# A DLRM tower on one core: gathers paced by a count of products, a fourth one-hot unit, fourteen units as pairs

## The chip, the cores and the metric

One core of one Trainium2 chip runs the whole program. The metric is the device time in microseconds (us), median of three runs.

## The reference, cut to what matters

```python
e = jnp.stack([tbl_f[ids[:, f]] for f in range(40)], axis=1)   # 512 x 40 x 64, float32
vi, vj = e[:, i_idx, :], e[:, j_idx, :]                        # all 780 pairs i < j
z = jnp.einsum('bpe,bpe->bp', jnp.einsum('bpd,pde->bpe', vi, W), vj)
h = jnp.concatenate([z, dense_ctx], axis=1)                    # 780 + 16
h = jnp.maximum(h @ W_top1 + b_top1, 0.0)                      # 512
h = jnp.maximum(h @ W_top2 + b_top2, 0.0)                      # 256
y = h @ W_top3
```

40 embedding tables, batch 512, 64 numbers a row. For each of the 780 pairs of fields, one field's vector goes through that pair's 64x64 matrix and is multiplied with the other's and summed. All is float32.

## The kernel before, in words

**Units and duos.** Two fields make a unit; `x[:, u, :]` holds unit u with its 2 x 64 numbers on the partitions and the batch along the row. The plan cuts the pairs into 196 duos, four to a round, 49 rounds (0 to 48). A duo is two 64-row matmuls side by side (TensorE, L443, written as four instructions; "four" duos at L434 as eight), a product by VectorE (L380, or L375 and L377 for a "four") into `prod`, and later a sum over partitions by TensorE (`sum_round`, L464) into `z_ps`. `sum_round` of a round comes two rounds late (`LAG`). Rounds 0 to 16 are pair rounds; from round 17 come the quad rounds, whose factor is `x_quad`, made by four ScalarE copies (L309) for each unit from `PAIRED` = 12 on. Rounds 23 and 39 are mixed ones. Each unit is made at a fixed duo (`transposed_at`): units 3 to 13 at duos 3, 7, 11, 16, 22, 30, 38, 47, 57, 60, 64, then 84, 88, 116, 120, 148, 152.

**How a unit is made.** Units 0 to 2 (`HOT_FIELDS`, small tables) come from one-hot products ahead of duo 0: VectorE compares the ids with the row numbers (L351, eight times for a unit), TensorE multiplies table and one-hot (L397, 32 instructions a unit) into `t_ps`, ScalarE copies it to `x` (L301). All three use the one bank `t_ps`, so each waits for the copy of the one before. The other 17 units are gathered: eight indirect DMAs of 128 rows for each, issued by GpSimd (L262), then four transposes (L411) into `t_ps` and the same copy.

**What sets GpSimd's order.** Its queue is written by hand. First it issues the gathers of units 3 to 15 one after the other, and at the first gather of a unit waits that the unit before has landed, and from unit 7 on that the slot of four is free (L261). From round 19 (`first_shared`) it issues two gathers for each round, and in 21 rounds (`plan.added`: 20, 22, 24, 26, 28, 30, 32, 34 to 38, 40 to 48) it adds products in pairs (L282, two instructions a round), after which `sum_round` takes four matmuls instead of eight.

**The rest.** SyncE loads the ids, the one-hot ids (`hot_ids_sb`, 512 KB a unit, by broadcast), `ident`, then the weights of every round (256 KB, eight slots; L242), from the third round on behind the first `x_ready`. ScalarE's queue loads the tables of the one-hot units (256 KB for each field, L290) and small things. At the end TensorE sums the last rounds, runs layer 1 (L474), layer 2 (L509) and the output (L515).

Of the kernel before, what the change touches and what calls it, by code (L numbers as in the profile page):

```python
# [6 lines left out]
I32 = mybir.dt.int32  # L7
# [6 lines left out]
DIM = 64  # L14
BATCH = 512
# [10 lines left out]
PROD_SLOTS = PROD_ROUNDS * ROUND  # L26

LAG = 2
GATHER_SLOTS = 4
W_SLOTS = 8  # L30

PAIRED = 12
QUADS = (UNITS - PAIRED) // 2
BLOCK_ROUNDS = QUAD // 4
DENSE_AT = 104

GATHERS_A_ROUND = 2


def pair_index(i, j):  # L40
# [1 line left out]

HOT_FIELDS = [2, 3, 4, 12, 17, 24]
HOT_UNITS = len(HOT_FIELDS) // 2

LANES = 128
HOT_SLOTS = 3
FIELD_ORDER = HOT_FIELDS + [f for f in range(FIELDS) if f not in HOT_FIELDS]  # L50


# [4 lines left out]
class Plan:  # L57
# [7 lines left out]
    def __init__(self):  # L65
        pairs = []
        for u in range(PAIRED):
            pairs += [("pair", k, u) for k in range(u)]
            if u % 4 == 3:
                pairs.append(("four", u - 3, u))  # L70
        full = len(pairs) // ROUND
        self.rounds = [pairs[i * ROUND:(i + 1) * ROUND] for i in range(full)]
        self.quad_start = []
        inside = pairs[full * ROUND:]
        for c in range(QUADS):
            u = PAIRED + 2 * c
# [16 lines left out]
        self.first_shared = self.quad_start[1] - 4  # L93

        left = CHUNKS * 2 * (UNITS - PAIRED - 4)
        self.added = []
        for r in range(self.first_shared, len(self.rounds)):
            left -= GATHERS_A_ROUND
            if self.is_quad(r) and (left <= 0 or (r - self.first_shared) % 2):
                self.added.append(r)  # L100

    def is_quad(self, r):
        return self.rounds[r][0][0] == "low"
# [40 lines left out]
def dlrm_tower(nc, ids, hot_ids, lane_rows, tables, w1_in, w2_in, head_in, dense_in, w_in, identity, selector, out):  # L144
# [7 lines left out]
    with ExitStack() as ctx:  # L152
# [13 lines left out]
        hot_ids_sb = sb("hot_ids_sb", [LANES, HOT_UNITS, 2, BATCH], I32)  # L166
        lane_rows_sb = sb("lane_rows_sb", [LANES, per_lane])
        hot_tables = sb("hot_tables", [LANES, HOT_UNITS, 2, per_lane * DIM])
# [4 lines left out]
        hot = x_quad[0:LANES, 2 * (QUADS - HOT_SLOTS):2 * QUADS, :]  # L173
# [5 lines left out]
        head = sb("head", [ROWS, M1 + 2 * M2])  # L179
        y_row = sb("y_row", [1, BATCH])  # L180

        h1 = [prod[:, m // 2, m % 2, :] for m in range(M1)]
        h2 = [prod[:, M1 // 2 + m // 2, m % 2, :] for m in range(M2)]
        b1, b2, w3 = head[:, 0:M1], head[:, M1:M1 + M2], head[:, M1 + M2:M1 + 2 * M2]
# [1 line left out]
        y_ps = psum("y_ps", [ROWS, DUO_SLOTS, 2, BANK])  # L186
        z_ps = psum("z_ps", [ROWS, BANK])
        t_ps = psum("t_ps", [ROWS, BANK])
        h1_ps = [t_ps[:, :], y_ps[:, 0, 0, :], y_ps[:, 0, 1, :], y_ps[:, 1, 0, :]]
        h2_ps = [y_ps[:, 1, 1, :], y_ps[:, 2, 0, :]]  # L190
        out_ps = y_ps[0:1, 2, 1, :]
# [5 lines left out]
        head_loaded = sem("head_loaded")  # L197
        w1_loaded = sem("w1_loaded")
        dense_loaded = sem("dense_loaded")
        lane_rows_loaded = sem("lane_rows_loaded")  # L200
        hot_ids_loaded = [sem(f"hot_ids_loaded{u}") for u in range(HOT_UNITS)]
        hot_tables_loaded = [sem(f"hot_tables_loaded{u}") for u in range(HOT_UNITS)]
# [22 lines left out]

        @block.sync
        def _(sp):
            sp.dma_start(ids_sb[:, :, :], ids).then_inc(ids_loaded, 16)
            for u in range(HOT_UNITS):
                sp.dma_start(hot_ids_sb[:, u, :, :],  # L230
                             hot_ids[u:u + 1, :, :].broadcast_to([LANES, 2, BATCH])).then_inc(hot_ids_loaded[u], 16)
                if u == 0:
                    sp.dma_start(ident[:, :], identity).then_inc(ident_loaded, 16)
            for r in range(len(plan.rounds)):
                slot = r % W_SLOTS
                if r == 2:

                    sp.wait_ge(x_ready, 1)
                if r >= W_SLOTS:

                    sp.wait_ge(y_ready, ROUND * (r - W_SLOTS + 1))
                sp.dma_start(w[:, slot, :, :], w_in[:, ROUND * r:ROUND * (r + 1), :]).then_inc(w_loaded[slot], 16)  # L242
            sp.wait_ge(out_ready, 1)
            sp.dma_start(out.rearrange("b o -> o b"), y_row[:, :]).then_inc(out_stored, 16)
            sp.wait_ge(out_stored, 16)

        @block.gpsimd
        def _(pool):
            pool.wait_ge(ids_loaded, 16)

            def gather(g):
# [15 lines left out]
            gathers = 2 * CHUNKS * UNITS  # L267
            g = 2 * CHUNKS * HOT_UNITS
            while g < 2 * CHUNKS * (PAIRED + 4):
                gather(g)  # L270
                g += 1
            for r in range(plan.first_shared, len(plan.rounds)):
                for _ in range(GATHERS_A_ROUND):
                    if g < gathers:
                        gather(g)
                        g += 1
# [7 lines left out]

        @block.scalar
        def _(act):
            act.dma_start(lane_rows_sb[:, :], lane_rows).then_inc(lane_rows_loaded, 16)
            for u in range(HOT_UNITS):
                for s, f in enumerate(fields_of(u)):
                    act.dma_start(hot_tables[:, u, s, :],  # L290
                                  tables[f]).then_inc(hot_tables_loaded[u], 16)
# [4 lines left out]
            def save_x(u):  # L296
                if u < HOT_UNITS:
                    act.wait_ge(hot_used, per_lane * (u + 1))
                else:
                    act.wait_ge(unit_transposed, u - HOT_UNITS + 1)  # L300
                nc.scalar.copy(x[:, u, :], t_ps[:, :]).then_inc(x_ready, 1)  # L301

                if u >= PAIRED:

# [37 lines left out]
        def _(dve):  # L342
            dve.wait_ge(lane_rows_loaded, 16)
            for u in range(HOT_UNITS):
                dve.wait_ge(hot_ids_loaded[u], 16)
                for q in range(per_lane):
                    n = per_lane * u + q
                    if n >= HOT_SLOTS:

                        dve.wait_ge(hot_used, n - HOT_SLOTS + 1)  # L350
                    nc.vector.tensor_scalar(hot[:, 2 * (n % HOT_SLOTS):2 * (n % HOT_SLOTS) + 2, :], hot_ids_sb[:, u, :, :],  # L351
                                            lane_rows_sb[:, q:q + 1], None, ALU.is_equal).then_inc(hot_ready, 1)
            have = {"x": 0, "quads": 0}
            for d, (kind, k, c) in enumerate(plan.duos):
# [31 lines left out]
        @block.tensor  # L386
        def _(pe):
            def pick_unit(u):
                pe.wait_ge(hot_tables_loaded[u], 32)
                if u:  # L390

                    pe.wait_ge(x_ready, u)
                for q in range(per_lane):
                    n = per_lane * u + q
                    pe.wait_ge(hot_ready, n + 1)
                    for s in range(2):
                        last = nc.tensor.matmul(t_ps[s * DIM:(s + 1) * DIM, :],  # L397
                                                hot_tables[:, u, s, q * DIM:(q + 1) * DIM],
                                                hot[:, 2 * (n % HOT_SLOTS) + s, :], start=q == 0, stop=q == per_lane - 1)
                    last.then_inc(hot_used, 1)  # L400

            def transpose_unit(u):
# [183 lines left out]
```

## Time and profile before

| | us |
|---|---|
| runs (three) | 389.33, 386.92, 388.93; median 388.93 |
| the profiled execution | 383.91 |
| its span, first to last instruction | 382.1 |
| TensorE busy | 339.4 (89%) |
| VectorE busy | 252.1 (66%) |
| GpSimd busy | 230.0 (60%) |
| ScalarE busy | 41.5 (11%) |

The span leaves out 1.8 us of the profiled execution. TensorE's records start when an instruction is handed to the engine, and their ends are modelled, so its busy time is no proof that it worked all that while. Idle time of an engine is put down to the engine that released it; "remote" stands where the profile shows no work that ended just before.

### The profile page before, as it was taken

To read this page: it belongs to the slowest core of one execution; us is meant where nothing else is said; L and a number is where in the kernel's file an instruction comes from. 1 tells how busy PE (TensorE), PEld (TensorE's weight loads), DVE (VectorE), ACT (ScalarE), POOL (GpSimd) and SP (SyncE) were. 2 spreads that over 40 slices of the span, in tenths; PEclk is the share of its full clock that TensorE was granted. 3 is DMA by queue.
4 is the path that set the end of the run, shared out by engine and by line. 5 is a ranking of instruction groups with operands and counts; after the bars stand their busy time and mean duration, and the time that the engine had idled before them with its cause. 6 is when DMAs were issued, how large, how long until landed. Compare 5 with 4: busy or idle time off the path is not lost.

```text
span 382.1 us, 4042 instructions
## 1 busy us (share of the span) xinstructions
PE 339.4 (89%) x1656; PEld 116.1 (30%) x1656; DVE 252.1 (66%) x225; ACT 41.5 (11%) x67; POOL 230.0 (60%) x182
## 2 busy tenths in 40 slices
PE   1999889886786398869999999999999999999997
PEld 0334223221221122312333233333333333333442
DVE  2686867664344276637887999889998999991000
ACT  1001000000000000312006000330006000001022
POOL 5586666766666651650017768878899499994000
PEclk9999999995868779998999999999999999999999
DMA  7551323222211273211211122222211210000000
GB/s 244 196 188 21 77 50 79 52 54 48 52 48 24 54 268 91 50 21 55 57 55 44 54 48 64 70 70 69 62 43 48 57 28 2 0 0 2 0 0 0
DMA packets 13764, 23.33 MB, mean 61 GB/s; under 512 B 3489, under 2 KB 3873, under 8 KB 13618
## 3 DMA queue, kind: packets, MB, share of 16 engines
q1 hardware_dynamic: 7778, 14.57, 13.0%
q0 software_dynamic: 4352, 4.47, 5.6%
q10 hardware_dynamic: 1616, 4.04, 3.0%
q8 instruction: 13, 0.21, 0.2%
q14 instruction: 5, 0.04, 0.0%
HBM read 23.06 MB, written 0.00 MB: 60 GB/s over the span
## 4 chain that ended last, share of the span: by engine, by line
PE 78%; POOL 7%; DVE 6%; another core or an unknown queue 4%; issue 3%; DMA 2%; ACT 0%; ACTq 0%; DVEq 0%
PE y_ps L443 41%; PE z_ps L464 18%; POOL prod L282 7%; PE t_ps L397 6%; PE y_ps L474 5%; DVE prod L380 4%; PE t_ps L411 2%; PE y_ps L434 2%; PE y_ps L509 2%; DMA hot_tables<-in_tbl 2%; PE t_ps L474 2%; DVE prod L377 1%; DVE prod L375 1%; PE y_ps L515 0%
## 5 line engine op out<-in xcount | busy, mean ns | idle before, releaser
L443 PE MATMUL y_ps<-x,w 64*128 64x512 f32 x768 | 190.5, 626 | 29.2 <-DVE prod L380 16.6
L262 POOL DMA_INDIRECT gathered<-in_tbl,ids_sb x136 | 131.8, 969 | 70.5 <-issue 35.7
L380 DVE TENSOR_TENSOR prod<-y_ps,x_quad 128x1024 f32<-128x1024 f32 x120 | 138.5, 1217 | 16.5 <-PE y_ps L443 14.5
L282 POOL TENSOR_TENSOR prod<-prod 128x1024 f32<-128x1024 f32 x42 | 98.0, 2359 | 47.7 <-DVE prod L380 47.1
L380 DVE TENSOR_TENSOR prod<-y_ps,x 128x1024 f32<-128x1024 f32 x72 | 84.9, 1220 | 60.2 <-PE y_ps L443 31.0
L443 PEld LDWEIGHTS y_ps<-x,w 64*128 64x128 f32 x768 | 69.4, 190 | 138.2 <-issue 93.2
L464 PE MATMUL z_ps<-prod,select 128*32 128x512 f32 x616 | 81.7, 639 | 0.2 <-POOL prod L282 0.2
L464 PEld LDWEIGHTS z_ps<-prod,select 128*32 128x32 f32 x616 | 15.6, 113 | 60.6 <-issue 45.8
L301 ACT COPY x<-t_ps 128x512 f32<-128x512 f32 x20 | 11.7, 585 | 200.3 <-PE t_ps L411 84.2
L397 PE MATMUL t_ps<-x_quad,hot_tables 128*64 128x512 f32 x96 | 23.5, 646 | 9.6 <-DMA hot_tables<-in_tbl 8.1
L351 DVE TENSOR_SCALAR x_quad<-hot_ids_sb,lane_rows_sb 128x1024 f32<-128x1024 int32 x24 | 18.3, 773 | 12.9 <-DMA hot_ids_sb<-hot_ids 7.2
L309 ACT COPY x_quad<-x 32x512 f32<-32x512 f32 x32 | 19.7, 616 | 0.5
L474 PE MATMUL y_ps<-zT,w 128*128 128x512 f32 (+1 forms) x42 | 18.5, 594 | 0.0
L397 PEld LDWEIGHTS t_ps<-x_quad,hot_tables 128*64 128x64 f32 x96 | 8.4, 149 | 23.8 <-issue 12.8
L315 ACT COPY zT<-z_ps 128x512 f32<-128x512 f32 x6 | 3.5, 585 | 102.2 <-PE z_ps L464 95.6
L411 PEld LDWEIGHTS t_ps<-ident,gathered 128*128 128x128 f32 x68 | 7.1, 140 | 13.7 <-issue 13.0
L411 PE MATMUL t_ps<-ident,gathered 128*128 128x128 f32 x68 | 11.2, 287 | 0.0
L474 PEld LDWEIGHTS y_ps<-zT,w 128*128 128x128 f32 (+1 forms) x42 | 7.9, 190 | 10.4 <-issue 10.4
L434 PE MATMUL y_ps<-x,w 64*64 64x512 f32 x32 | 7.7, 601 | 0.7 <-DVE prod L377 0.7
L375 DVE TENSOR_TENSOR prod<-y_ps,x 64x1024 f32<-64x1024 f32 x4 | 4.9, 1214 | 3.7 <-PE y_ps L434 2.0
L474 PE MATMUL t_ps<-zT,w 128*128 128x512 f32 (+1 forms) x14 | 6.4, 597 | 0.8 <-ACT zT L315 0.8
L509 PE MATMUL y_ps<-prod,w 128*128 128x512 f32 x16 | 7.0, 592 | 0.0
(17 smaller groups left out, 22.3 us busy)
## 6 DMA issues: line engine op xcount, KB each, us to landing
w<-w_rows SPq DMA_DIRECT2D x49, 256.0 KB
gathered<-in_tbl,ids_sb POOLq DMA_INDIRECT x136
w<-w_rows ACTq DMA_DIRECT2D x1, 1792.0 KB
hot_tables<-in_tbl ACTq DMA_DIRECT2D x6, 256.0 KB
hot_ids_sb<-hot_ids SPq DMA_DIRECT2D x3, 512.0 KB
w<-w_rows ACTq DMA_DIRECT2D x1, 512.0 KB
ids_sb<-ids_rows SPq DMA_DIRECT2D x1, 80.0 KB, 2.1
ident<-identity SPq DMA_DIRECT2D x1, 64.0 KB
```

The lines of the kernel that those rows point to most:

```text
L262: nc.gpsimd.indirect_dma_start(gathered[:, slot, c, s * DIM:(s + 1) * DIM], None, tables[f][:, :], bass.IndirectOffsetOnAxis(ap=ids_sb[:, ...
L282: nc.gpsimd.tensor_tensor(prod[:, low, :, :], prod[:, low, :, :], prod[:, high, :, :], ALU.add).then_inc(added, 1)
L309: last = nc.scalar.copy(x_quad[n * QUAD:(n + 1) * QUAD, u - PAIRED - u % 2 + h, :], x[s * DIM + h * QUAD:s * DIM + (h + 1) * QUAD, u, :])
L351: nc.vector.tensor_scalar(hot[:, 2 * (n % HOT_SLOTS):2 * (n % HOT_SLOTS) + 2, :], hot_ids_sb[:, u, :, :], lane_rows_sb[:, q:q + 1], None, ...
L380: nc.vector.tensor_tensor(prod[:, d % PROD_SLOTS, :, :], y_ps[:, d % DUO_SLOTS, :, :], factor, ALU.mult).then_inc(prod_ready, 1)
L397: last = nc.tensor.matmul(t_ps[s * DIM:(s + 1) * DIM, :], hot_tables[:, u, s, q * DIM:(q + 1) * DIM], hot[:, 2 * (n % HOT_SLOTS) + s, :], ...
L411: last = nc.tensor.transpose(t_ps[:, c * ROWS:(c + 1) * ROWS], gathered[:, u % GATHER_SLOTS, c, :], ident[:, :])
L434: last = nc.tensor.matmul(y_ps[side * DIM:(side + 1) * DIM, d % DUO_SLOTS, half, :], w[rows, r % W_SLOTS, d % ROUND, half * DIM:(half + 1) ...
L443: last = nc.tensor.matmul(y_ps[:, d % DUO_SLOTS, half, :], w[rows, r % W_SLOTS, d % ROUND, :], x[rows, u, :], start=True, stop=True)
L464: last = nc.tensor.matmul(z_ps[q * QUAD:(q + 1) * QUAD, :], select[:, 1 if quad else 0, QUAD - row:2 * QUAD - row], prod[:, d % PROD_SLOTS ...
L474: last = nc.tensor.matmul(h1_ps[m], w1[rows, b, m * ROWS:(m + 1) * ROWS], zT[rows, b, :], start=(b == 0), stop=(b == NBLK - 1))
L509: last = nc.tensor.matmul(h2_ps[m], w2[:, k, m * ROWS:(m + 1) * ROWS], h1[k], start=(k == 0), stop=(k == M1 - 1))
```

## The change

- GpSimd: the wait on the unit before goes. The plan gives each gather a count of products (`gather_times`), and it waits for that count (`prod_ready`). 24 gathers (units 4 to 6) have count 0; then follow counts 1 to 9, 11 to 19 and so on, about nine gathers for ten products, up to count 81, then one for every second product up to 143. There are six slots for gathered units instead of four. Gathers: 128 instead of 136.
- One-hot: units 0 to 3. Units 0 to 2 are summed in banks of `y_ps`, unit 3 in `t_ps`, so none waits for a copy; duo 1 waits for three copies. Eight one-hot slots instead of three; these, the one-hot ids and the tables now lie in `prod`.
- First loads: the ids move to ScalarE's queue; the tables of unit 0 come in two halves; both queues wait until the first one-hot ids have landed before they load for units 1 to 3.
- `PAIRED` = 14: rounds 17 to 22 are pair rounds too; the quad rounds start at 23. There are 49 rounds as before. Units 12 and 13 are made at duos 69 and 81, unit 3 ahead of duo 0, the others where they were. `plan.added` has 18 rounds: 25, 27, 29, 31, 33, 35 to 38, 40 to 48.
- End: the first five blocks of layer 1 run ahead of the wait for the sixth.

```diff
-GATHER_SLOTS = 4
+GATHER_SLOTS = 6
-PAIRED = 12
+PAIRED = 14
-GATHERS_A_ROUND = 2
+GATHER_LEAD = 8
+GATHERED_FIRST = 3
-HOT_FIELDS = [2, 3, 4, 12, 17, 24]
+HOT_FIELDS = [2, 3, 4, 12, 17, 24, 27, 28]
-HOT_SLOTS = 3
+HOT_SLOTS = 8
...
+    def gather_times(self):
+        parts = 2 * CHUNKS
+        after = [0] * parts * GATHERED_FIRST
+        first = HOT_UNITS + GATHERED_FIRST
+        due = [max(0, self.transposed_at(u) - GATHER_LEAD) for u in range(first, UNITS)]
+        at, u = 0, first
+        while u < UNITS:
+            pace = [(due[v - first] - at) / (v + 1 - u) for v in range(u, UNITS)]
+            step = min(pace)
+            end = u + pace.index(step)
+            for n in range(parts * (end + 1 - u)):
+                after.append(1 + int(at + step * n / parts))
+            at, u = due[end - first], end + 1
+        return after
...
+        hot = [prod[:, n, :, :] for n in range(HOT_SLOTS)]
+        hot_tables = [prod[:, PROD_SLOTS - 1 - u, :, :] for u in range(HOT_UNITS)]
...
+        hot_ps = [y_ps[:, 2, 0, :], y_ps[:, 2, 1, :], y_ps[:, 1, 0, :], t_ps[:, :]][4 - HOT_UNITS:]
...
                 if u == 0:
-                    sp.dma_start(ident[:, :], identity).then_inc(ident_loaded, 16)
+                    sp.wait_ge(hot_ids_loaded[0], 16)
+            sp.dma_start(ident[:, :], identity).then_inc(ident_loaded, 16)
...
-                if part == 0 and HOT_UNITS < u < PAIRED + 4:
-                    before = (u - 1 - HOT_UNITS) // GATHER_SLOTS + 1
-                    pool.wait_ge(unit_gathered[(u - 1) % GATHER_SLOTS], 16 * 2 * CHUNKS * before)
+                if plan.gather_after[g - first]:
+                    pool.wait_ge(prod_ready, plan.gather_after[g - first])
...
+            first = 2 * CHUNKS * HOT_UNITS
+            g = first
+            for r in range(len(plan.rounds)):
+                while g - first < len(plan.gather_after) and plan.gather_after[g - first] < ROUND * (r + 1):
+                    gather(g)
+                    g += 1
...
+            act.dma_start(ids_sb[:, :, :], ids).then_inc(ids_loaded, 16)
             act.dma_start(lane_rows_sb[:, :], lane_rows).then_inc(lane_rows_loaded, 16)
+            half = per_lane // 2 * DIM
+            for s, f in enumerate(fields_of(0)):
+                act.dma_start(hot_tables[0][:, s, :half], tables[f][:, :half]).then_inc(first_half_loaded, 16)
+            for s, f in enumerate(fields_of(0)):
+                act.dma_start(hot_tables[0][:, s, half:], tables[f][:, half:]).then_inc(hot_tables_loaded[0], 16)
+            act.wait_ge(hot_ids_loaded[0], 16)
...
-                if u:
-                    pe.wait_ge(x_ready, u)
...
+                if d == 1:
+                    need = max(need, HOT_UNITS - 1)
...
             pe.wait_ge(w1_loaded, 32)
+            layer1(0, range(NBLK - 2))
             pe.wait_ge(z_saved, NBLK - 1)
-            layer1(0, range(NBLK - 1))
+            layer1(0, [NBLK - 2])
```

## Rows read from the trace of the kernel before

**Rows 1.** The page: the chain that ended last, shares of the span by engine.
```profile
PE 78%; POOL 7%; DVE 6%; another core or an unknown queue 4%; issue 3%; DMA 2%; ACT 0%; ACTq 0%; DVEq 0%
```
**Rows 2.** Busy time by stage: stretch and length, engines, PEclk, DMA share, GB/s.
```profile
33.00:66.00 33.00, 29.84 (x158) 10.68 (x156) 24.66 (x22) 2.93 (x5) 21.09 (x23) 1.00 0.27 64
66.00:101.00 35.00, 29.10 (x142) 8.58 (x140) 19.32 (x17) 1.17 (x2) 23.11 (x25) 0.85 0.19 46
101.00:126.00 25.00, 18.03 (x74) 4.68 (x72) 10.55 (x9) 1.17 (x2) 16.71 (x19) 0.80 0.21 54
126.00:153.00 27.00, 19.20 (x97) 5.99 (x96) 14.23 (x13) 0.59 (x1) 12.99 (x14) 0.81 0.41 136
153.00:178.00 25.00, 19.60 (x106) 6.18 (x103) 14.04 (x12) 6.68 (x11) 11.32 (x12) 0.93 0.20 47
178.00:316.00 138.00, 137.26 (x762) 48.14 (x764) 121.53 (x106) 20.64 (x34) 92.06 (x57) 1.00 0.20 53
```
**Rows 3.** Timeline, transposes and their copies: start, length, engine; in brackets idle before.
```profile
126.09 0.66 PE L411 MATMUL t_ps<-ident,gathered 128*128 128x128 f32 x4
135.16 0.59 ACT L301 COPY x<-t_ps 128x512 f32<-128x512 f32 x1 [19.46 <-remote]
152.69 0.66 PE L411 MATMUL t_ps<-ident,gathered 128*128 128x128 f32 x4
153.38 0.58 ACT L301 COPY x<-t_ps 128x512 f32<-128x512 f32 x1 [17.64 <-PE t_ps L411]
199.88 0.66 PE L411 MATMUL t_ps<-ident,gathered 128*128 128x128 f32 x4
200.58 0.58 ACT L301 COPY x<-t_ps 128x512 f32<-128x512 f32 x1 [16.44 <-PE t_ps L411]
```
**Rows 4.** Timeline of GpSimd: gathers and additions, picked from four places.
```profile
24.81 1.34 POOL L262 DMA_INDIRECT gathered<-in_tbl,ids_sb  x1 [0.30 <-issue]
...
132.03 0.94 POOL L262 DMA_INDIRECT gathered<-in_tbl,ids_sb  x1 [0.30 <-issue]
...
154.12 0.94 POOL L262 DMA_INDIRECT gathered<-in_tbl,ids_sb  x1 [8.55 <-PE t_ps L411]
...
229.11 0.96 POOL L262 DMA_INDIRECT gathered<-in_tbl,ids_sb  x1
...
234.35 4.70 POOL L282 TENSOR_TENSOR prod<-prod 128x1024 f32<-128x1024 f32 x2 [0.54 <-DVE prod L380]
```
**Rows 5.** The waits, whole span: who waited for whom, total, times, longest.
```profile
DVE prod L380 <- remote: 26.2, 13, 6.6
```
**Rows 6.** The chain that ended last, in order of time: start, length, what.
```profile
8.11 9.32 PE t_ps L397 x32
17.43 0.72 issue
18.15 7.09 PE t_ps L397 x32
...
33.05 2.78 PE y_ps L443 x12
...
178.00 3.63 PE y_ps L443 x16
181.63 1.85 PE z_ps L464 x16
...
210.25 0.99 PE z_ps L464 x8
...
315.95 27.92 POOL prod L282 x12
...
345.04 0.59 ACT zT L315
```
**Rows 7.** The timeline of VectorE at the start.
```profile
7.21 2.08 DVE L351 TENSOR_SCALAR x_quad<-hot_ids_sb,lane_rows_sb 128x1024 f32<-128x1024 int32 x3 [7.21 <-DMA hot_ids_sb<-hot_ids]
```
**Rows 8.** Busy time by stage, the first 10 us; columns as in rows 2.
```profile
0.00:10.00 10.00, 1.89 (x6) 0.75 (x8) 2.08 (x3) 1.28 (x1) 5.54 (x10) 1.00 0.78 252
```

More of the change, by code:

```diff
@@ L91, in __init__ @@
         self.tail_rows = 4 * (len(self.rounds) - BLOCK_ROUNDS * (self.blocks - 1))
-        self.first_shared = self.quad_start[1] - 4
-        left = CHUNKS * 2 * (UNITS - PAIRED - 4)
+        self.gather_after = self.gather_times()
         self.added = []
-        for r in range(self.first_shared, len(self.rounds)):
-            left -= GATHERS_A_ROUND
-            if self.is_quad(r) and (left <= 0 or (r - self.first_shared) % 2):
+        for r in range(self.quad_start[0] + 2, len(self.rounds)):
+            gathers = any(after >= ROUND * r for after in self.gather_after)
+            if self.is_quad(r) and (not gathers or r % 2):
                 self.added.append(r)
+    def gather_times(self):
[12 more added lines that the diff above has]
+        return after
     def is_quad(self, r):
@@ L165, in dlrm_tower @@
         per_lane = lane_rows.shape[1]
-        hot_ids_sb = sb("hot_ids_sb", [LANES, HOT_UNITS, 2, BATCH], I32)
         lane_rows_sb = sb("lane_rows_sb", [LANES, per_lane])
-        hot_tables = sb("hot_tables", [LANES, HOT_UNITS, 2, per_lane * DIM])
         gathered = sb("gathered", [ROWS, GATHER_SLOTS, CHUNKS, 2 * DIM])
@@ L171, in dlrm_tower @@
         x_quad = sb("x_quad", [ROWS, 2 * QUADS, BATCH])
-        hot = x_quad[0:LANES, 2 * (QUADS - HOT_SLOTS):2 * QUADS, :]
         w = sb("w", [ROWS, W_SLOTS, ROUND, ROWS])
@@ L180, in dlrm_tower @@
         y_row = sb("y_row", [1, BATCH])
+        hot = [prod[:, n, :, :] for n in range(HOT_SLOTS)]
+        hot_tables = [prod[:, PROD_SLOTS - 1 - u, :, :] for u in range(HOT_UNITS)]
+        hot_ids_sb = [prod[:, PROD_SLOTS - 1 - HOT_UNITS - u, :, :].bitcast(I32) for u in range(HOT_UNITS)]
         h1 = [prod[:, m // 2, m % 2, :] for m in range(M1)]
@@ L199, in dlrm_tower @@
         dense_loaded = sem("dense_loaded")
+        first_half_loaded = sem("first_half_loaded")
         lane_rows_loaded = sem("lane_rows_loaded")
@@ L227, in _ @@
         def _(sp):
-            sp.dma_start(ids_sb[:, :, :], ids).then_inc(ids_loaded, 16)
             for u in range(HOT_UNITS):
-                sp.dma_start(hot_ids_sb[:, u, :, :],
+                sp.dma_start(hot_ids_sb[u],
                              hot_ids[u:u + 1, :, :].broadcast_to([LANES, 2, BATCH])).then_inc(hot_ids_loaded[u], 16)
                 if u == 0:
-                    sp.dma_start(ident[:, :], identity).then_inc(ident_loaded, 16)
+                    sp.wait_ge(hot_ids_loaded[0], 16)
+            sp.dma_start(ident[:, :], identity).then_inc(ident_loaded, 16)
             for r in range(len(plan.rounds)):
@@ L265, in gather @@
                 ).then_inc(unit_gathered[slot], 16)
[L267 to L276, printed above, removed]
+            first = 2 * CHUNKS * HOT_UNITS
[4 more added lines that the diff above has]
+                    g += 1
                 if r in plan.added:
@@ L286, in _ @@
         def _(act):
+            act.dma_start(ids_sb[:, :, :], ids).then_inc(ids_loaded, 16)
             act.dma_start(lane_rows_sb[:, :], lane_rows).then_inc(lane_rows_loaded, 16)
-            for u in range(HOT_UNITS):
+            half = per_lane // 2 * DIM
[4 more added lines that the diff above has]
+            act.wait_ge(hot_ids_loaded[0], 16)
+            for u in range(1, HOT_UNITS):
                 for s, f in enumerate(fields_of(u)):
-                    act.dma_start(hot_tables[:, u, s, :],
-                                  tables[f]).then_inc(hot_tables_loaded[u], 16)
+                    act.dma_start(hot_tables[u][:, s, :], tables[f]).then_inc(hot_tables_loaded[u], 16)
             act.dma_start(select[:, :, :], selector).then_inc(select_loaded, 16)
@@ L300, in save_x @@
                     act.wait_ge(unit_transposed, u - HOT_UNITS + 1)
-                nc.scalar.copy(x[:, u, :], t_ps[:, :]).then_inc(x_ready, 1)
+                nc.scalar.copy(x[:, u, :], hot_ps[u] if u < HOT_UNITS else t_ps[:, :]).then_inc(x_ready, 1)
                 if u >= PAIRED:
@@ L350, in _ @@
                         dve.wait_ge(hot_used, n - HOT_SLOTS + 1)
-                    nc.vector.tensor_scalar(hot[:, 2 * (n % HOT_SLOTS):2 * (n % HOT_SLOTS) + 2, :], hot_ids_sb[:, u, :, :],
+                    nc.vector.tensor_scalar(hot[n % HOT_SLOTS], hot_ids_sb[u],
                                             lane_rows_sb[:, q:q + 1], None, ALU.is_equal).then_inc(hot_ready, 1)
@@ L388, in pick_unit @@
             def pick_unit(u):
-                pe.wait_ge(hot_tables_loaded[u], 32)
-                if u:
-                    pe.wait_ge(x_ready, u)
                 for q in range(per_lane):
                     n = per_lane * u + q
+                    if u:
+                        if q == 0:
+                            pe.wait_ge(hot_tables_loaded[u], 32)
+                    elif q % (per_lane // 2) == 0:
+                        pe.wait_ge(first_half_loaded if q == 0 else hot_tables_loaded[0], 32)
                     pe.wait_ge(hot_ready, n + 1)
                     for s in range(2):
-                        last = nc.tensor.matmul(t_ps[s * DIM:(s + 1) * DIM, :],
-                                                hot_tables[:, u, s, q * DIM:(q + 1) * DIM],
-                                                hot[:, 2 * (n % HOT_SLOTS) + s, :], start=q == 0, stop=q == per_lane - 1)
+                        last = nc.tensor.matmul(hot_ps[u][s * DIM:(s + 1) * DIM, :],
+                                                hot_tables[u][:, s, q * DIM:(q + 1) * DIM],
+                                                hot[n % HOT_SLOTS][:, s, :], start=q == 0, stop=q == per_lane - 1)
                     last.then_inc(hot_used, 1)
```

## The prediction, on record before the changed kernel was run

> **What bounds the kernel now.** I read the chain of waits first: TensorE carries 78% of it, GpSimd 7%, "another core or an unknown queue" 4%, on a kernel that runs on one core [rows 1]. So TensorE is the engine, and something that the profile can't name holds it up. The table by stage shows where. From 178 to 316 us TensorE is busy 137.26 of 138 us at full clock. From 33 to 178 us it isn't: VectorE makes 22 products in the first 33 us, then 17 in 35, 9 in 25, 13 in 27 and 12 in 25 us, and the granted clock falls to 0.80 to 0.93 of full [rows 2]. These are the 68 duos of rounds 0 to 16 (two of them take two instructions, and one that crosses a border counts on both sides), over 145 us: 2.1 us a duo.
>
> What a duo should cost stands in the chain: a round of four takes 3.63 us of duos and 1.85 us of sum (1.00 us where GpSimd has added) [rows 6], so 5.48 us, 1.37 us a duo, and 0.6 us for each unit transposed.
>
> The third view is the timeline of transposes and copies. Unit 10's transposes were handed over at 126.09 and should end at 126.75; the copy that waits for nothing but them starts at 135.16, 8.4 us late, marked "remote". Unit 11's copy starts 0.03 us after its transposes end, unit 14's 0.04 us [rows 3]. VectorE has 13 such waits, 26.2 us [rows 5]. So what TensorE signals arrives late in this stage. GpSimd's timeline says when: around unit 10 it issues gathers back to back, 0.94 us each and 0.30 between them, 1.25 us from one to the next; before unit 11's copy it had stood still for 8.55 us; after 200 us, where unit 14 is made, gathers come in fours between additions [rows 4]. My reading: long runs of gathers at 1.25 us delay TensorE's signals, VectorE then starts late, TensorE waits, and its clock drops on top. The lost time is 178.00 - 33.05 = 144.9 us for rounds 0 to 16 [rows 6], against a clean sum of 17 x 3.63 + 15 x 1.85 + 9 x 0.6 (units 3 to 11) + the 1.3 us of units 12 and 13 = 96.2 us. Some 49 us are lost there. That is the pot.
>
> One rule of the Trainium skill speaks against this. "SBUF — State Buffer", section "SBUF: two separate sides", says that engine ports and DMA ports are disjoint and that TensorE never waits on anyone; and "Perfetto Trace Analysis", section on the profiler window of each engine, says that TensorE's end is an estimate. By these the lateness would be TensorE working slowly for reasons of its own, not the gathers' doing. The trace neither agrees nor refutes: no row shows TensorE's true end. It is the first rival below.
>
> **The change, step by step,** on the profiled execution (span 382.1).
>
> 1. *Start.* VectorE begins at 7.21, when the first one-hot ids land [rows 7], TensorE at 8.11 [rows 6]. In the first 10 us 252 GB/s are moved [rows 8]. In the queues until then are now only 512 KB of ids for unit 0, its tables (512 KB, two halves) and 80 KB of ids for the gathers: 1.1 MB at 252 GB/s is 4.4 us, from about 1.5 us on (two issues of 0.4 us, and the way to the first bytes, an estimate). I take TensorE's start at 6.0: -2.1. Bounds: 0 (the two queues are limited one by one) and -3. Units 1 to 3 (3 MB) follow from 6 us on, by 252 GB/s until 18 us, the first of them by 10 to 11, while TensorE needs them at 15, 22 and 29: hidden.
>
> 2. *One-hot units.* First unit 9.32 us, of which about 2.2 at half clock (a warm one takes 7.09) [rows 6]; three more at 7.0 (the gap of 0.72 us before each, a wait for the copy, goes, and 0.1 of fill). Duo 0 starts at 6.0 + 9.3 + 21 = 36.3 instead of 33.05: +3.3 with the start counted in. VectorE's comparisons (three in 2.08 us [rows 7]) keep ahead of the 0.86 us that TensorE takes for each. The wait for three copies at duo 1 costs nothing: the third copy is over 7 us before, hidden by unit 3.
>
> 3. *Rounds 0 to 16.* Clean: 17 x 3.63 + 15 x 1.85 + 8 transposed units (4 to 11) x 0.6 = 94.3. VectorE needs 121.53 / 106 = 1.15 us for a product [rows 2]; in the first three rounds no sums give it time to catch up (12 x 1.15 = 13.8 against 3 x 3.63 = 10.9 us: +2.9; the second product instruction of a "four" is taken up by the sums). Round 17 would start at 36.3 + 97.2 = 133.5, not 178.00.
>
> 4. *Do the new gathers leave TensorE's signals alone?* Nine gathers for ten products of 1.43 us (1.37, and a transposed unit every ten) is one for each 1.59 us on average, and none can run ahead: where signals are late, products are late, and GpSimd pauses. Inside a round the products come at 1.15 us, so up to four gathers follow at 1.25 and then GpSimd rests about 1 us. The trace has no such pattern for long. Nearest rows: with VectorE comparing, a gather takes up to 1.34 us and more, and in that stage TensorE runs its 7.09 us a unit without a hitch [rows 4, 6]; and fours of gathers between additions leave the copies punctual [rows 3, 4]. From below 0; from above the pace of 33 to 66 us, with pauses only after eight gathers: 33 us for what should take 29, so +4 there and about +12 over 68 duos. I take +2, since both near rows show none.
>
> 5. *The gathers as a resource.* 1.25 us each against 1.59 us of room, landing eight products (11 us) ahead of use: hidden. The 24 free ones run beside the one-hot units: 3.1 + 24 x 1.4 = 37 us, just as that phase ends. If this cover went, a late unit would stop TensorE for 1.25 us a missing gather.
>
> 6. *From round 17 on.* Before, 382.1 - 178.0 = 204.1. Pair or quad, a duo costs TensorE the same. Three rounds fewer are added by GpSimd: 3 x (1.85 - 1.00) = +2.6. Units 12 and 13 are now transposed inside it: +1.2. GpSimd between 23 and 35: two gathers a round at 2.5 and an addition of 4.70 [rows 4] every other round are 9.7 us of the 10.1 us that two rounds take. A gather now waits for its product and an addition queues behind it, so an addition ends up to 1.3 us later; TensorE asks for it two rounds later: 0 (bounds 0 and +3). The end stays: nine rounds of additions in a row, GpSimd's last 27.92 us on the chain [rows 6], as before. Layer 1's first five blocks now cover the copy of 0.59 us and its signal [rows 6]: -0.8.
>
> Sum: 133.5 + 2 + 204.1 + 2.6 + 1.2 - 0.8 = 342.6. The profiled execution lies 1.8 us above its span, and the median 5.0 above the profiled one. That spread I put down to the late signals, which differ from run to run; as they go I keep 1.6 of it. Forecast: 346.
>
> **Rivals.**
>
> *A. The lateness isn't the gathers' doing (ends slower).* It belongs to TensorE in pair rounds; quad rounds are clean because they are quad rounds. For it: every late signal before 178 us falls in a pair round, and from round 17, the first quad one, none is late [rows 2, 3]. Against: unit 11 is punctual in a pair round, just where GpSimd stands still [rows 3, 4]. Price: six more pair rounds, 24 duos, at 2.1 instead of 1.37 us (+18; at the 2.2 us of 66 to 153 us, +20), and +3.3 at the start, +2.6 + 1.2 - 0.8: 388.9 + 6.3 + 19 = about 414. It decides as soon as products 12 to 68 still come at over 2 us each.
>
> *B. Gathers at nine for ten products are still too dense.* Lateness as in 33 to 66 us, over the whole stage: +12 instead of +2, 356. For it: GpSimd is 80% busy there, as before. Against: the average of 1.59 us, and the pauses.
>
> *C. As B, but growing,* as before after 66 us, checked only by the pauses: half the pot stays, 24 us: 346 + 24 = 370, up to 385. For it: before, lateness grew from one stage to the next, with the clock [rows 2].
>
> *D. GpSimd is the new bound late,* its additions pushed behind waiting gathers: +3 in all, 346 to 352; inside the range.
>
> **How the numbers follow.** Forecast 0.64, B 0.16, C 0.11, A 0.06; 0.03 for an end near 389 in which C and the dearer start cancel. The likeliest gives 346, its own range 339 (start -3, no lateness, nothing kept of the spread) to 352. B reaches 360; with part of C the range 339 to 364 leaves out some 0.18. A measurement of this kernel can tell about 1% from no change (its three runs lie 0.6% apart). Faster by over 1%: 0.91; within 1%: 0.03; slower: 0.06.
>
> **What would show it.** Products 0 to 68 at 1.4 to 1.45 us each, full clock from the first 15 us to the end, copies starting within 0.1 us of their transposes, no "remote" waits on VectorE or ScalarE: step 4 right. Round 17 near 135 us: steps 1 to 3 right. TensorE starting at 6.0 and duo 0 at 36 us. After it 207 us to the end. I am wrong if copies in rounds 3 to 16 are still some us late although gathers pause (A), if they are late only after runs of gathers (B, C), or if the start isn't earlier.

## The result, and the profile after

The changed kernel takes 354.72 us (median of six, 349.35 to 356.18) against 386.93 us before (six, 382.46 to 389.33): ratio 0.912, 95% interval 0.901 to 0.923. The forecast was 346.0, the range 339 to 364. The gain is 32 us where 43 were forecast. The profiled execution took 351.68 us, its span is 349.7.

The page of the kernel after, the chain that ended last by engine, against [rows 1]:

```profile
PE 83%; POOL 8%; DVE 5%; issue 2%; DMA 1%; ACT 0%; DVEq 0%
```

"Another core or an unknown queue" (4% before) is gone. The busy time by stage of the kernel after, columns as in [rows 2]:

```profile
0.00:36.00 36.00, 27.89 (x116) 8.93 (x116) 21.40 (x30) 2.46 (x3) 24.65 (x27) 1.00 0.64 201
36.00:66.00 30.00, 28.09 (x136) 9.39 (x136) 22.12 (x21) 2.93 (x5) 16.20 (x17) 1.00 0.23 55
66.00:106.00 40.00, 39.59 (x230) 13.35 (x232) 33.15 (x29) 2.35 (x4) 22.39 (x24) 1.00 0.26 65
106.00:145.00 39.00, 38.02 (x218) 13.10 (x216) 28.19 (x25) 1.46 (x3) 22.06 (x24) 1.00 0.42 123
145.00:180.00 35.00, 33.65 (x198) 11.49 (x196) 28.77 (x25) 7.57 (x13) 15.07 (x16) 1.00 0.24 59
180.00:285.00 105.00, 105.00 (x584) 36.78 (x582) 93.20 (x81) 13.96 (x23) 76.93 (x50) 1.00 0.21 55
```

VectorE makes 29 products in the 40 us from 66, where it made 17 in 35 and then 9 in 25 before. The granted clock is 1.00 in every stretch, where it was 0.80 to 0.93 from 66 to 178. That is where the time was won: rounds 0 to 16 take 101.4 us instead of 144.9. One stage is worse than forecast, and it is the first. The timeline of that stage of the kernel after, one-hot comparisons, products and copies, and the last unpaced gather, picked:

```profile
23.83 0.75 DVE L376 TENSOR_SCALAR prod<-prod,lane_rows_sb 128x1024 f32<-128x1024 int32 x1 [0.67 <-PE y_ps L423]
...
25.28 0.59 ACT L326 COPY x<-y_ps 128x512 f32<-128x512 f32 x1 [9.44 <-PE y_ps L423]
...
28.77 1.04 PE L423 MATMUL t_ps<-prod 128*64 128x512 f32 x4
29.56 0.75 DVE L376 TENSOR_SCALAR prod<-prod,lane_rows_sb 128x1024 f32<-128x1024 int32 x1 [2.02 <-PE y_ps L423]
...
30.37 1.08 PE L423 MATMUL t_ps<-prod 128*64 128x512 f32 x4 [0.56 <-DVE prod L376]
...
37.18 1.13 POOL L284 DMA_INDIRECT gathered<-in_tbl,ids_sb  x1 [0.30 <-issue]
38.17 0.59 ACT L326 COPY x<-y_ps 128x512 f32<-128x512 f32 x1 [12.31 <-PE t_ps L423]
40.11 0.59 ACT L326 COPY x<-t_ps 128x512 f32<-128x512 f32 x1 [1.35 <-PE t_ps L423]
```

A comparison needs a slot that TensorE has released. Eight of them take 5.40 us when nothing stops them; here, from 19.5 us on, nearly all come 1.4 us apart, each waiting for TensorE, and from 30 us on TensorE then waits for each. Unit 3's products, into `t_ps`, were begun at 28.77, so unit 2's had been handed over by then; its copy starts at 38.17, over 9 us later. All 24 unpaced gathers lie in this stage, and the last runs from 37.18 to 38.31. Unit 3's copy, at 40.11, is punctual again. So late signals turned up in a stage where the kernel before had none, and duo 0 came at 40.0 instead of 36.3.

In the rounds the copies behind the transposes are late by 2.1 us (unit 5), 1.2 (unit 6), 1.1 (unit 9), under 0.9 for the rest; before it was 8.4 for unit 10 [rows 3], and 3.9, 6.1 and 5.3 for units 8, 9 and 13. The kernel after, timeline, units 5 and 8:

```profile
52.85 0.66 PE L437 MATMUL t_ps<-ident,gathered 128*128 128x128 f32 x4
55.59 0.59 ACT L326 COPY x<-t_ps 128x512 f32<-128x512 f32 x1 [6.45 <-remote]
...
84.02 0.66 PE L437 MATMUL t_ps<-ident,gathered 128*128 128x128 f32 x4
84.72 0.59 ACT L326 COPY x<-t_ps 128x512 f32<-128x512 f32 x1 [12.19 <-PE t_ps L437]
```

Round 17 starts at 141.4 (178.0 before), the end follows 208.3 us later. The chain at the end, against [rows 6]: layer 1 starts without a gap, where the copy of 0.59 us stood on the chain.

```profile
284.34 27.92 POOL prod L300 x12
...
312.30 1.07 PE z_ps L493 x8
313.37 5.35 PE t_ps L503 x12
```

### The profile page after: what moved, and what is told of

Its sections match the earlier page's. It is cut to its first block, busy times and chain, and to the rows that moved or that the text cites. A ratio compares the mean times of both kernels' runs of the same rounds, so it can differ in the third digit from the quotient of the medians.

```text
span 349.7 us, 4138 instructions
## 1 busy us (share of the span) xinstructions
PE 334.5 (96%) x1708; PEld 116.2 (33%) x1708; DVE 255.6 (73%) x233; ACT 36.6 (10%) x59; POOL 209.2 (60%) x168
## 4 chain that ended last, share of the span: by engine, by line
PE 83%; POOL 8%; DVE 5%; issue 2%; DMA 1%; ACT 0%; DVEq 0%
PE y_ps L472 41%; PE z_ps L493 20%; POOL prod L300 8%; PE y_ps L423 7%; PE y_ps L503 5%; DVE prod L405 3%; PE t_ps L437 2%; PE t_ps L423 2%; PE y_ps L539 2%; PE t_ps L503 2%; PE y_ps L463 2%; DMA prod<-hot_ids 1%; DVE prod L376 1%; DVE prod L402 1%; PE y_ps L545 1%
## 5 line engine op out<-in xcount | busy, mean ns | idle before, releaser
L284 POOL DMA_INDIRECT gathered<-in_tbl,ids_sb x128 | 124.9, 976 | 101.1 <-DVE prod L405 56.1
L472 PE MATMUL y_ps<-x,w 64*128 64x512 f32 x768 | 181.7, 606 | 3.7 <-DVE prod L405 2.1
L405 DVE TENSOR_TENSOR prod<-y_ps,x 128x1024 f32<-128x1024 f32 x96 | 111.5, 1218 | 27.7 <-PE y_ps L472 17.6
L405 DVE TENSOR_TENSOR prod<-y_ps,x_quad 128x1024 f32<-128x1024 f32 x96 | 110.8, 1217 | 10.8 <-PE y_ps L472 9.3
L300 POOL TENSOR_TENSOR prod<-prod 128x1024 f32<-128x1024 f32 x36 | 84.1, 2373 | 6.3 <-DVE prod L405 6.1
L376 DVE TENSOR_SCALAR prod<-prod,lane_rows_sb 128x1024 f32<-128x1024 int32 x32 | 23.0, 756 | 16.0 <-PE y_ps L423 6.2
L423 PE MATMUL y_ps<-prod 128*64 128x512 f32 x96 | 22.7, 636 | 6.2 <-DVE prod L376 6.2
L334 ACT COPY x_quad<-x 32x512 f32<-32x512 f32 x24 | 14.8, 616 | 0.4
L423 PEld LDWEIGHTS y_ps<-prod 128*64 128x64 f32 x96 | 7.8, 148 | 20.2 <-issue 12.6
L423 PE MATMUL t_ps<-prod 128*64 128x512 f32 x32 | 8.6, 614 | 2.7 <-DVE prod L376 2.7
```

The costliest lines, as they stand in the source:

```text
L284: nc.gpsimd.indirect_dma_start(gathered[:, slot, c, s * DIM:(s + 1) * DIM], None, tables[f][:, :], bass.IndirectOffsetOnAxis(ap=ids_sb[:, ...
L300: nc.gpsimd.tensor_tensor(prod[:, low, :, :], prod[:, low, :, :], prod[:, high, :, :], ALU.add).then_inc(added, 1)
L334: last = nc.scalar.copy(x_quad[n * QUAD:(n + 1) * QUAD, u - PAIRED - u % 2 + h, :], x[s * DIM + h * QUAD:s * DIM + (h + 1) * QUAD, u, :])
L376: nc.vector.tensor_scalar(hot[n % HOT_SLOTS], hot_ids_sb[u], lane_rows_sb[:, q:q + 1], None, ALU.is_equal).then_inc(hot_ready, 1)
L405: nc.vector.tensor_tensor(prod[:, d % PROD_SLOTS, :, :], y_ps[:, d % DUO_SLOTS, :, :], factor, ALU.mult).then_inc(prod_ready, 1)
L423: last = nc.tensor.matmul(hot_ps[u][s * DIM:(s + 1) * DIM, :], hot_tables[u][:, s, q * DIM:(q + 1) * DIM], hot[n % HOT_SLOTS][:, s, :], st ...
```

## The experiments

The runs went to chips on which the kernel before takes one of two quite different times. Each result names its own before, run on the same chip at the same time. The first measurement above doesn't name its chip.

| kernel | chips 9, 5: us, ratio | chips 3, 8 and the first measurement: us, ratio |
|---|---|---|
| before | 351.2 to 351.8 | 385.3 to 389.0 |
| before, gathers free | | 401.5, 1.043 |
| before, gathers paced | 339.2, 0.963 | 363.0, 0.938 |
| after | 343.8, 0.978 | 354.7, 0.912 |
| after, gathers free | 343.2, 0.974; 343.1, 0.976 | |
| after, `PAIRED` 12 | 342.1, 0.972 | |
| after, three one-hot units | 337.0, 0.957 | |
| after, both of these | | 363.4, 0.941 |
| after, 16 free gathers, spread | 344.7, 0.981 | |

**After without its product waits (chip 9).**

```diff
-                if plan.gather_after[g - first]:
-                    pool.wait_ge(prod_ready, plan.gather_after[g - first])
```

> The changed kernel, but no gather waits for a count of products; GpSimd issues them back to back (1.25 us apart) as far as the six slots allow. Theory G (long runs of gathers delay TensorE's signals, pauses clear them): rounds 0 to 16 go back from 101 us to 130 us or more, copies start 3 to 9 us after their transposes, the granted clock falls below 1.0, the time is 380 to 400 us. Theory P (the lateness belongs to TensorE in pair rounds, the other parts of the change brought the gain): no change, 352 to 358 us.

343.16 us, ratio 0.974 (0.972 to 0.977), every copy right behind its transposes, though GpSimd issues 108 gathers in a row. My theory missed by some 40 us. It had to be asked first whether this chip shows late signals at all; the forecasts of the other three runs made with it on chip 9, further down, took that for granted too.

**Before and after again (chip 9).**

> The kernel before itself, for its trace beside the others of this chip. Theory C, on a chip without late signals: rounds 0 to 16 still cost more than the clean 96 us, because GpSimd needs 11.4 to 11.8 us for each gathered unit (eight gathers and the wait for the landing) and units 12 and 13 are due at duos 60 and 64, before their gathers have landed: TensorE waits for the gathers of units 12 and 13, 6 to 9 us in all, and the clock drops there. On a chip with late signals: the trace of before again.

> The changed kernel itself. In the first four runs the kernel before took 351.8 us where it had taken 386.9, and no copy was late in any of them: the late signals of TensorE belong to the chip on which a kernel runs as well as to the gathers. Theory C (chip-bound lateness): where the kernel before takes about 352 us, this one takes 341 to 345 us with a one-hot phase of 30 us and all copies within 0.1 us; where it takes about 387, this one takes 350 to 356. Theory N (the first pair of measurements was an accident of its time, and the changed kernel always takes 350 to 356 us): 350 us or more.

Before takes 351.3 us, not 387, and no wait is put down to "remote". After takes 343.75, ratio 0.978 (0.975 to 0.981). That is theory C in both, and not N. A repeat of the free version gave 342.4, and one on chip 5 343.12, ratio 0.976 (0.973 to 0.979):

> After without its waits on the count of products, nothing else changed: what is left of the change when only the pacing is gone. Tested so far only where no signal of TensorE came late (343.2 against 343.75, no difference). Where the before kernel takes some 387 us: theory of the gathers (unbroken runs delay TensorE's signals) expects 380 us or more, ratio over 0.98, as the before kernel without pacing took 401.5; units' copies 5 us and more behind their last transpose through rounds 0 to 16. Rival, that in the changed kernel the fourth one-hot unit and the banks give enough cover without pacing: at most 365 us, ratio under 0.95. Where the before kernel takes 351 us: 343 again, and nothing new.

So on these chips no signal is late, and the change gains some 2% by other means. The page of before on chip 9, its chain, tells what bounds it there:

```profile
PE 50%; POOL 32%; issue 12%; DMA 3%; DVE 2%; ACT 0%; POOLq 0%
```

The same run: a line of its waits, the busy time from 120 to 147 us, and the timeline of units 12 and 13, transposes and the first gather of the unit behind:

```profile
PE t_ps L411 <- DMA gathered<-in_tbl,ids_sb: 8.1, 3, 3.8
...
120.00:147.00 27.00, 20.61 (x102) 7.71 (x100) 12.55 (x12) 6.09 (x10) 17.92 (x19) 0.81 0.23 53
...
125.29 1.12 PE L411 MATMUL t_ps<-ident,gathered 128*128 128x128 f32 x4 [2.57 <-DMA gathered<-in_tbl,ids_sb]
125.51 0.94 POOL L262 DMA_INDIRECT gathered<-in_tbl,ids_sb  x1 [1.79 <-DMA gathered<-in_tbl,ids_sb]
...
136.70 1.12 PE L411 MATMUL t_ps<-ident,gathered 128*128 128x128 f32 x4 [3.82 <-DMA gathered<-in_tbl,ids_sb]
136.91 0.94 POOL L262 DMA_INDIRECT gathered<-in_tbl,ids_sb  x1 [1.72 <-DMA gathered<-in_tbl,ids_sb]
```

A unit costs GpSimd 136.91 - 125.51 = 11.4 us: eight gathers at 1.25 and a wait for their landing. TensorE needs eleven units in 64 duos, one for each 8.6 us by the costs of the prediction, so GpSimd's lead runs out: TensorE waits for rows at unit 7 (1.7 us) and, at the end of the stage, at units 12 (2.6) and 13 (3.8). Around these waits its granted clock is 0.81 (120 to 147 us), and the round behind unit 13 takes 5.73 us instead of 3.63.

**Before with only the pacing, chip 9, then chip 8.** Six slots, the gathers in the order and with the counts of `gather_times` for three one-hot units (46 gathers with counts 1 to 40, behind 24 free ones; after has 36 behind 24), no wait for the unit before to land:

```diff
-GATHER_SLOTS = 4
+GATHER_SLOTS = 6
...
-                if part == 0 and HOT_UNITS < u < PAIRED + 4:
-                    before = (u - 1 - HOT_UNITS) // GATHER_SLOTS + 1
-                    pool.wait_ge(unit_gathered[(u - 1) % GATHER_SLOTS], 16 * 2 * CHUNKS * before)
+                if plan.gather_after[g - first]:
+                    pool.wait_ge(prod_ready, plan.gather_after[g - first])
```

> The kernel before, with one part of the change alone: six slots, and each gather waits for its count of products; three one-hot units, twelve paired units, the old first loads. Theory G: rounds 0 to 16 fall from 145 us to 97 to 105 us, the time to 340 to 350 us, as low as the changed kernel or lower, since the fourth one-hot unit cost TensorE 7 us. Theory P: 383 to 390 us, as before.

> The kernel before with six slots and the product waits, no landing waits: the same kernel as the one that took 339.2 us where nothing is late, and the free-running one that took 401.5 beside a before of 385.3 plus the product waits. It tells whether the pacing alone carries the measured gain where the before kernel takes some 385 us. Theory of the gathers (unbroken runs of them delay TensorE's signals, product waits stop that): at most 358 us, ratio at or under 0.93, and in rounds 0 to 16 no copy more than some 2 us behind its last transpose. Rival, that the gain of the change came from its other parts (the fourth one-hot unit, fourteen paired units, the banks): at least 375 us, ratio over 0.97, with waits for unknown signals as in the free version. Where the before kernel takes 351 us: 339 again, and neither theory is tested.

Chip 9: 339.2 us, ratio 0.963 (0.960 to 0.965), where theory G said 340 to 350, but not for its reason: no signal was late. The landing waits go, and TensorE waits for no rows: 12 us, more than the whole change brings there. Chip 8: 363.0 us, ratio 0.938 (0.929 to 0.947), between what the two theories expected (at most 358, at least 375) and nearer to the first. The pacing carries some 26 us there, where the whole change brought 32 in the first measurement. Of the 26, chip 9 shows 12 without any lateness; some 14 are lateness gone, and 24 us of it stay (363.0 against 339.2). Nor are all copies within 2 us: unit 9's is 3.3 us late, unit 4's 7.1. The timeline there, units 4 and 5, with two gathers:

```profile
41.02 0.66 PE L425 MATMUL t_ps<-ident,gathered 128*128 128x128 f32 x4
46.71 0.94 POOL L280 DMA_INDIRECT gathered<-in_tbl,ids_sb  x1 [0.30 <-issue]
48.74 0.58 ACT L315 COPY x<-t_ps 128x512 f32<-128x512 f32 x1 [11.66 <-remote]
...
51.74 0.94 POOL L280 DMA_INDIRECT gathered<-in_tbl,ids_sb  x1 [4.09 <-DVE prod L394]
53.53 1.12 PE L425 MATMUL t_ps<-ident,gathered 128*128 128x128 f32 x4
54.68 0.58 ACT L315 COPY x<-t_ps 128x512 f32<-128x512 f32 x1 [5.36 <-PE t_ps L425]
```

32 gathers in a row end at 47.65 us. Unit 4's transposes fall near the end of that run, and their copy is 7.1 us late. After a pause of 4 us a shorter run begins at 51.74; unit 5's transposes fall two gathers into it, and their copy is punctual.

**The same without the product waits (chip 3).** The kernel before with six slots; GpSimd stops only where no slot is free. Against the paced version the product waits go, and the gathers of units 16 to 19 stand where they stood before, two a round from round 19 on:

```diff
-                if plan.gather_after[g - first]:
-                    pool.wait_ge(prod_ready, plan.gather_after[g - first])
```

> The kernel before, with the six slots and the product waits of the paced version taken out again, and without the wait for each unit's gathers to land: GpSimd issues freely until it meets the free-slot wait. What tells pacing from the landing waits. Theory of landing waits (GpSimd's waits of 1.4 to 2.2 us for landing, some 17 of them, set the start of units in the undisturbed trace): the same 338 to 341 us as the paced version's 339.2, TensorE waiting for no gathered rows, since both drop those waits. Theory of pacing (counting products is what helps): within 2 us of before, 350. Theory that unbroken gathers delay TensorE's signals, where the before kernel takes some 387 us: at least 380, units' copies 5 us or more behind their last matmul in rounds 0 to 16; where before takes 351 us, no such copy is seen and this theory says nothing.

401.5 us, ratio 1.043 (1.034 to 1.052), beside a before of 385.3: slower than before, as the theory of unbroken gathers said, though only two copies, of units 4 and 5, are over 5 us late. Busy time by stage:

```profile
36.00:66.00 30.00, 13.29 (x54) 4.66 (x50) 10.72 (x10) 1.17 (x2) 22.68 (x25) 0.71 0.20 44
66.00:106.00 40.00, 11.88 (x32) 2.64 (x32) 4.13 (x5) 0.59 (x1) 23.84 (x26) 0.54 0.13 28
106.00:145.00 39.00, 35.25 (x180) 10.99 (x180) 26.15 (x23) 1.76 (x3) 20.80 (x22) 0.90 0.22 52
```

The timeline of the same run, unit 5, two products, and GpSimd's last free gather and the first behind its pause:

```profile
58.06 1.11 PE L407 MATMUL t_ps<-ident,gathered 128*128 128x128 f32 x4
...
75.70 1.22 DVE L376 TENSOR_TENSOR prod<-y_ps,x 128x1024 f32<-128x1024 f32 x1 [9.28 <-remote]
...
86.51 0.94 POOL L258 DMA_INDIRECT gathered<-in_tbl,ids_sb  x1 [0.30 <-issue]
86.90 1.23 DVE L376 TENSOR_TENSOR prod<-y_ps,x 128x1024 f32<-128x1024 f32 x1 [9.97 <-remote]
...
93.20 0.59 ACT L297 COPY x<-t_ps 128x512 f32<-128x512 f32 x1 [42.85 <-remote]
93.43 0.95 POOL L258 DMA_INDIRECT gathered<-in_tbl,ids_sb  x1 [5.97 <-remote]
```

This is the pattern with nothing that holds the gathers back. GpSimd issues 64 of them in a row until 87.5 us. VectorE gets five products in the 40 us from 66, one about every ten, each behind a "remote" wait; unit 5's copy is 34 us late; the mean granted clock drops to 0.54, so for most of the stretch it is at the lower of its two levels, 1.2 GHz. From 87.5 us on the gathers meet the free-slot wait and come in eights with pauses, and from 106 us 23 products come in 39 us. The waits of this run, whole span, against [rows 5] (26.2 us before):

```profile
ACT x L297 <- remote: 65.5, 3, 42.9
DVE prod L376 <- remote: 53.7, 8, 10.0
```

Against the paced version (363.0) that is 38 us more, and all of it lies in rounds 0 to 16: from duo 0's product to duo 68's 161.4 us pass here and 123.4 there, and from then to the end 203.0 in both, so the other place of the late gathers costs nothing. The two ran on different chips, whose before (385.3 and 389.0) differ by 4 us, and the other way.

**After with three one-hot units (chip 9), with 12 paired units (chip 9), with both (chip 3).**

```diff
-HOT_FIELDS = [2, 3, 4, 12, 17, 24, 27, 28]
+HOT_FIELDS = [2, 3, 4, 12, 17, 24]
...
-PAIRED = 14
+PAIRED = 12
```

> The changed kernel with three one-hot units instead of four: 7 us of TensorE less, eight gathers more, so that the first 24 gathers fall into a one-hot phase of 23 instead of 34 us. In the changed kernel the one-hot phase took 33.8 us for a clean 30, and from 19.5 us on every comparison waited for TensorE. Theory G: one-hot phase about 24 us, some lateness moves into the first rounds: 347 to 355 us. Theory P: 347 to 349 us.

> The changed kernel with twelve units as pairs instead of fourteen: six pair rounds fewer, gathers one a product instead of nine for ten, two more rounds with additions. Theory G: the gathers are a little denser (1.43 instead of 1.59 us), some more lateness, less 1.7 us for the additions: 353 to 362 us. Theory P: six late pair rounds fewer, faster: 345 to 352 us.

> After with three one-hot units and twelve paired units, both together. If the two prices add, as they should when they lie in different stretches: after less 6.8 (fourth one-hot unit) less 1.6 (two more summed rounds) = 335.3 us where after takes 343.7. If they overlap, because the gathers bound the rounds again: 337, no better than with three one-hot units alone, and TensorE waits for gathered rows reappear in units 7 to 13. Where the before kernel takes 387 us: below after by 8 us or more if one-hot cost is TensorE work, less if the lateness decides.

Three one-hot units: 336.97 us, ratio 0.957 (0.955 to 0.960), the best seen on chip 9, and below both forecasts; the fourth costs 6.8 us there, all of its TensorE time, and buys nothing. `PAIRED` 12: 342.1, ratio 0.972 (0.969 to 0.975), 1.6 us below after, which is the price of two more rounds that GpSimd adds; again below both forecasts. Both on chip 3: 363.4, ratio 0.941 (0.929 to 0.952), which is above the 0.912 of after, so the two parts together bring something where signals are late; what each brings was not run there. The kernel without them has the first loads, banks and layer 1 of the change, and still only equals the paced version of before (0.938). So those edits bring nothing measurable there, and the last 3% (of some 387, about 10 us, each ratio known to about 1%) belong to the fourth one-hot unit and the fourteen pairs. They cost 8.4 us on chip 9, yet lateness, taken as the time above the same kernel on chip 9, falls from 24 us in the paced before to 11 in after (36 in before). What both change is the pace: 46 gathers with counts up to 40 with neither, 42 without the fourth unit, 40 with `PAIRED` 12, 36 in after. That the pace is the cause is argued, not shown; no run changed it alone on such a chip. The one-hot stage of the version with neither is late too, timeline of that run:

```profile
31.27 3.55 PE L472 MATMUL y_ps<-x,w 64*128 64x512 f32 x11
...
39.53 0.58 ACT L326 COPY x<-t_ps 128x512 f32<-128x512 f32 x1 [9.50 <-remote]
39.66 3.49 DVE L405 TENSOR_TENSOR prod<-y_ps,x 128x1024 f32<-128x1024 f32 x3 [9.46 <-remote]
```

**After with 16 free gathers, spread over the one-hot stage (chip 9).** It was meant for the lateness of the first stage, but ran on a chip that has none:

```diff
-GATHER_LEAD = 8
+GATHER_LEAD = 4
...
-GATHERED_FIRST = 3
+GATHERED_FIRST = 2
...
+                if 0 < g - first < 2 * CHUNKS * GATHERED_FIRST:
+                    pool.wait_ge(hot_ready, (g - first) * per_lane * HOT_UNITS // (2 * CHUNKS * GATHERED_FIRST))
```

> The changed kernel with 16 gathers instead of 24 ahead of the first product, each of them behind a count of one-hots (one for two), and a lead of 4 instead of 8 duos. Where signals are late, theory G: the one-hot phase falls from 33.8 to 30 us, 3 to 4 us faster than the changed kernel. Where they are not: the same time within 1 us, if a lead of 4 duos (5.7 us) still covers the landing.

344.7 us, ratio 0.981 (0.978 to 0.984): 1 us above after, most of it from round 17 on. With the shorter lead the last gather has count 147, the plan no longer lets GpSimd add round 36, and a round that isn't added costs 0.85 us more. Whether it wins where signals are late stays open, as does how free gathers in the changed kernel do there.

## Why the prediction was right, and where it was off

**Steps 1 to 3 and 6, the clean terms: right within 1.5 us each.** After on chip 9 has none of the lateness and shows them bare. Its chain:

```profile
6.75 22.59 PE y_ps L423 x96
29.34 6.87 PE t_ps L423 x32
36.21 3.63 PE y_ps L472 x16
```

TensorE starts at 6.75 (forecast 6.0; 6.22 in the first measurement), duo 0 at 36.2 (36.3), round 17 at 134.9 (133.5, or 135.5 with the 2 us of step 4), the end 206.8 us later (207.1): span 341.7 against 342.6. Some of this is luck: the later start is made up by one-hot units that are shorter than forecast, and step 3 priced all duos alike, while on this chain a "four" takes 1.9 us and any other duo 0.91. Two of them lie in rounds 0 to 16, 2 us that the sum lacks, and the 2.9 us for VectorE were some 0.5 too many.

**Step 2 was the step that failed**, in the sentence that comparisons "keep ahead" of TensorE. It took the one-hot stage to stay punctual because it had been before [rows 4, 6]. Measured: from 19.5 us on the comparisons wait for TensorE, unit 2's copy is over 9 us late, and duo 0 comes at 40.0, +3.7. Step 4 asked for lateness only behind product waits; the 24 free gathers ahead of them had been costed at nothing (step 5).

**Step 4: the direction is shown, the size was too small, and its reason is half shown.** Rounds 0 to 16 took 141.4 - 40.0 = 101.4 us where 97.2 + 2 were allowed: +2.2. The rest of the 8.7 us: 1.2 from round 17 on; 0.2 outside the span; 1.4 between the profiled execution and the median (3.0, where 1.6 was kept). The spread didn't go: six runs lie 2% apart, those on chip 9 0.3%, so it may well belong to the lateness that stayed. By its own signs step 4 is not met in full: copies are up to 2.1 us late, and one wait of ScalarE (6.4 us) and one of VectorE (1.1) are put down to "remote". That product waits help where signals are late, runs on chips 3 and 8 show; that nine gathers for ten products leave so little lateness where the denser pace left 24 us is seen, but why is not tested, and no run took the waits out of the changed kernel on such a chip.

**The pot of 49 us was read as one thing, and is two.** On chip 9, with nothing late, before still needs from duo 0 to round 17 some 112 us (to 145.3) against the clean 96.2 + 2.9: about 13 us come from GpSimd's own bound, eight gathers and a landing wait for each unit: 8.1 us of waits for rows and the lower clock around them. The paced before shows it, with 12 us less on that chip. The profile of before hid that, because late signals slowed the products more. The change takes away this part whole and most of the other, so the sum came near by luck for a quarter of the pot: its reason was wrong there.

**Rival A is out:** rounds 17 to 22 are pair rounds now, at a clock of 1.00, and take 36.2 us in the first measurement and 36.0 on chip 9, 1.5 us a duo and not 2.1; and chip 9 runs all pair rounds clean. **B gives 356**, near what was measured, but by lateness of 12 us in the rounds; they had 4, and the one-hot stage, which B doesn't name, as much. That 355 lies next to B's number doesn't speak for B. **C and D** didn't come: step 6 holds within 1.2 us.

**Whether the gathers delay TensorE's signals.** On chips 3 and 8: yes, in that without the product waits rounds 0 to 16 take 38 us more, and VectorE's waits put down to "remote" are 53.7 us instead of 9.3. On chips 9 and 5: no, with 108 gathers in a row. What differs between the chips no profile shows. The rule that the prediction cites against its reading ("SBUF — State Buffer" in the Trainium skill, section "SBUF: two separate sides": engine and DMA ports are separate, TensorE's port waits on no one) says nothing of the way by which signals travel. Chip 9 agrees with it (343.2 us free, 343.75 paced); on chips 3 and 8 gathers do make TensorE's results come late, and no run shows whether over a port. Whether its work or its signal is late, and whether it is GpSimd's issuing or the transfers themselves that do it, stays open.

## What to carry to other kernels

Pace a long series of gathers by the progress of their consumer rather than by their own landing: put into the kernel before, it gained 3.8% where nothing was late (no landing waits) and 6.2% where signals were. Before a theory of contention is tested, look whether the chip of the run shows the symptom at all: run the kernel before, and look for "remote" waits. A part that pays on one chip can cost on another: the fourth one-hot unit and the fourteen pairs together gained some 10 us where signals are late and cost 8.4 (6.8 and 1.6) on chip 9.

## What the runs showed that was not expected

The same kernel takes 351 us on chips 9 and 5 and 385 to 389 on chips 3 and 8, at a spread of under 1% on the former and up to 3% on the latter.

Unbroken gathers alone don't suffice, even on a late chip. In the free version on chip 3 they run from 3.15 us, and the copies of units 0 to 3 are punctual until 37.5 us; at that time a gather takes 1.49 us on average (17 intervals from 8.68 to 33.98), stretched beside the comparisons. Where the one-hot stage is late it is 1.40 (after: 20 intervals from 9.19 to 37.18) and 1.35 (both parts undone: 20 from 9.24 to 36.31), and in the rounds of the free version 1.25. It fits a limit on the rate of gathers, but late comparisons themselves let gathers run faster, so cause and effect aren't told apart. In both late stages comparisons and gathers keep one pace: in after a comparison starts at 32.46, 33.88, 35.31 and 36.74 and a gather 0.40 to 0.45 us behind each. A rival to the rate stands untested: the two kernels whose one-hot stage is late have the new stage (eight slots, a bank for each unit), and the three that ran on such chips with the old one (three slots, a wait for every copy) are punctual there, two of them with unbroken gathers.
